# The third value tile, the first queries' load, the bias rows and the order of evictions in the first layer of a two-layer cross-attention kernel

## The chip, the cores and the metric

The kernel runs on one core of a Trainium2 chip. The metric is the device time of one launch in microseconds, lower is better. Five engines work side by side, each with its own queue of instructions in program order: PE (TensorE, matrix products and transposes), ACT (ScalarE), DVE (VectorE), POOL (GpSimd) and SP (SyncE), which here only issues the DMA transfers. They wait for each other on semaphores.

## The reference

Eight batches of 112 query rows and 375 context rows, 512 features each, go through two layers. The change lies wholly in the first, L0:

```
h  = layer_norm(x, ln1_w, ln1_b)
q, k, v = h @ q_w + q_b, ctx @ k_w + k_b, ctx @ v_w + v_b     # 16 heads of 32
o  = softmax(mask(q k^T / sqrt(32))) @ v
x  = x + o @ cproj_w + cproj_b
x  = x + gelu(layer_norm(x, ln2_w, ln2_b) @ fc_w + fc_b) @ proj_w + proj_b
```

The second layer, L1, has 16 heads of 128, two cross-attentions over the same context with one extra key each, and an MLP of its own. All is in f32.

## The kernel before, in words

**Products.** Every product of two f32 matrices is three matmuls (`product`, L1630 to L1632): each operand is kept as a high half (rounded) and a low half (what the rounding left), and high·high, high·low and low·high are summed in PSUM. So each operand that an engine makes is written twice: ACT evicts a PSUM bank with the bias into the `_hi` tile, then DVE computes the `_lo` tile from the same bank and the `_hi` tile. Names: `w_a`, `w_b` weights (slots 0 and 1, loaded into `w_raw_a`, `w_raw_b` in four columns of 128), `cs` the context, `k` a key tile, `v` the values, `act_t` the transposed activations, `x` the rows of the residual (seven tiles of 128).

**Start.** `ln` measures, scales and turns the rows of x. PE meanwhile computes value tiles 0 and 1 of batch 0. Then `query` computes the queries in eight steps i (four columns of the weights, for the first half of the rows and then the second), each evicted by ACT and stored to DRAM by SP (`q_scratch`); from there the queries of each batch are loaded back in another layout. SP, ACT and DVE all have part of that load: SP issues it (L601), ACT makes `q_hi` (L939), DVE makes `q_lo` (L1305). In the `prologue` of the first attention PE computes key tile 0, value tile 2 and key tile 1 of batch 0, the scores of tile 0 and a value tile of batch 1.

**The attention of layer 0** (`attend_first`) runs over eight batches b and four tiles t (four heads each). Everything is software-pipelined by hand. In tile t PE computes the scores of tile t+1 (`score_quad`), and then for each head j = 0 to 3 transposes the probabilities of tile t (`turn`, L1751, into the one bank ps_t) and computes a piece of the keys of tile t+2 or of the values of the next batch (table `FILL`; `FILL_FIRST` in batch 0). At the end comes probabilities times values for the four heads (`weighted`, L1763). ACT evicts each transpose (`turned`, L953), takes the exponential for tile t+1 (`exp`, L957), evicts the key tile (`key_hi`, L947), value tile (`value_out`, L934) and output (`output_hi`, L963). DVE takes scores, mask and maximum (`masked_maximum`, L1336), normalises (`normalized_0`: L1310 and L1313), and makes `k_lo` (`key_lo`, L1319) and the output's low half (L1346). Once a batch, in tile 2, DVE rounds the context of the batch after the next (`context_hi`) and POOL makes its low half in four instructions (`context_lo`, L797).

What each wait is: a `turn` waits until `turned` of the head before it has emptied the bank; `weighted` waits for `turned` of head 3; `score_quad` waits for `key_lo` of its tile and the four maxima of the tile before; key tile 1 waits for `key_lo` of key tile 0, since both use bank ps_k.

The last batch (b = 7) has no next batch to compute keys and values for after tile 1. ACT splits the four columns of the output weights there (`w_b_hi`, POOL makes `w_b_lo`), and PE fills in the first five row tiles of the output projection.

**The tail** (`project` with layer 0) computes row tiles 5 and 6 of the projection, adds to x (`add_y`, L1509), measures, scales (`scale` on DVE, L1199 and L1209), turns (`turn_row`, L1640) and scales the seven rows by the second layer norm (`scaled` on ACT, L878, `halves` on DVE, L1215 and L1217), up to where the MLP starts (`up`). In the last batch the columns of the MLP's first weights (block A_M0) are split as well (`split_hi` on ACT L863, `split_lo` on DVE L1180).

POOL adds the output bias to x (`ln`, L791) as seven instructions in one go after the first layer norm. SP's queue after the last batch: the next block of `w_raw_a`, each column when the same column's `w_lo` is made (`load_block`, L523), then `w_raw_b` for the MLP, the context by key (L714) and the next bias row.

## Time and profile before

| | us |
|---|---|
| median of three runs | 2335.46 (2335.41 to 2336.28) |
| the profiled execution | 2335.53 |
| its span, first to last instruction | 2333.7 |
| PE busy | 2281.2 (98%) |
| DVE busy | 1335.6 (57%) |
| ACT busy | 1123.3 (48%) |
| POOL busy | 366.1 (16%) |

All that the change touches lies in the first 335 us or so of the span. A row of the timeline gives start and duration in us, the engine, the line and operation, output and inputs, and in brackets how long the engine was idle before it and who released it.

### The profile page before, as it was taken

How to read it: one execution, taken by the hardware profiler on the slowest of the kernel's cores; microseconds unless marked ns; L12 is line 12 of the kernel's file. 1: busy time of each engine (PE TensorE's matmuls, PEld its weight loads, DVE VectorE, ACT ScalarE, POOL GpSimd, SP SyncE). 2: the span in 40 equal slices, each digit the busy share in tenths (PEclk: the TensorE clock that was granted, in tenths of full speed). 3: DMA queues.
4: the chain of work that ended last, by engine and by line, in shares of the span. 5: the costliest groups of instructions: out<-in, count | busy, mean ns of one | idle time of the engine just before them, and what ended most of it. 6: DMA issues, size and time to landing. Idle time of an engine off the chain costs nothing.

```text
span 2333.7 us, 37085 instructions
## 1 busy us (share of the span) xinstructions
PE 2281.2 (98%) x13091; PEld 2069.4 (89%) x13091; DVE 1335.6 (57%) x3098; ACT 1123.3 (48%) x2468; POOL 366.1 (16%) x731
## 2 busy tenths in 40 slices
PE   6999899999999999999999999999999999999999
PEld 5777778888999999999998898999999999988887
DVE  6777784443656556655654625665565565554743
ACT  4777762354445445444443434445445444452421
POOL 2111126530000100100101120001001001003421
PEclk9999999999999999999999999999999999999999
DMA  5422126575455645645645474545555555544210
GB/s 180 141 74 71 59 82 229 177 241 144 161 185 196 211 153 197 233 143 193 224 148 164 148 218 153 192 159 193 213 182 182 202 191 190 182 149 139 60 55 32
DMA packets 255224, 376.25 MB, mean 161 GB/s; under 512 B 90302, under 2 KB 210514, under 8 KB 255042
## 3 DMA queue, kind: packets, MB, share of 16 engines
q1 hardware_dynamic: 255042, 373.87, 47.4%
q8 instruction: 108, 1.77, 0.3%
q14 instruction: 74, 0.61, 0.1%
HBM read 315.77 MB, written 58.05 MB: 160 GB/s over the span
## 4 chain that ended last, share of the span: by engine, by line
PE 91%; DVE 3%; ACT 3%; issue 2%; DMA 1%; POOL 0%; SPq 0%; ACTq 0%; DVEq 0%
PE ps_k L1630 10%; PE ps_k L1631 10%; PE ps_k L1632 10%; PE ps_o L1630 8%; PE ps_o L1632 8%; PE ps_o L1631 8%; PE ps_v L1630 6%; PE ps_v L1632 6%; PE ps_v L1631 6%; PE ps_s L1630 4%; PE ps_s L1632 4%; PE ps_s L1631 4%; PE ps_t L1814 3%; PE ps_t L1751 1%; PE ps_o L1763 1%
## 5 line engine op out<-in xcount | busy, mean ns | idle before, releaser
L1630 PE MATMUL ps_k<-cs_hi,w_a_hi 128*128 128x376 f32 x1152 | 390.3, 339 | 3.9 <-DVE k_lo L1405 3.7
L1631 PE MATMUL ps_k<-cs_lo,w_a_hi 128*128 128x376 f32 x1152 | 385.2, 334 | 0.0
L1632 PE MATMUL ps_k<-cs_hi,w_a_lo 128*128 128x376 f32 x1152 | 384.2, 334 | 0.0
L1038 ACT ACTIVATE prob<-ps_s,row_columns 112x376 f32<-112x376 f32 x256 | 147.4, 576 | 304.9 <-DVE row_columns L1411 304.8
L815 POOL CAST k_hi<-xk_hi 128x1 fp32r<-128x1 f32 x256 | 47.4, 185 | 1233.0 <-PE ps_s L1632 1233.0
L1630 PEld LDWEIGHTS ps_k<-cs_hi,w_a_hi 128*128 128x128 f32 x1152 | 216.8, 188 | 7.5 <-issue 6.8
L1631 PEld LDWEIGHTS ps_k<-cs_lo,w_a_hi 128*128 128x128 f32 x1152 | 217.1, 188 | 0.5
L1632 PEld LDWEIGHTS ps_k<-cs_hi,w_a_lo 128*128 128x128 f32 x1152 | 216.9, 188 | 0.0
L1405 DVE SCALAR_TENSOR_TENSOR k_lo<-ps_k,col_b,k_hi 128x375 fp32r<-128x375 f32 x256 | 155.2, 606 | 79.1 <-ACT k_hi L1007 73.5
L1007 ACT ACTIVATE k_hi<-ps_k,col_b 128x375 fp32r<-128x375 f32 x256 | 146.4, 572 | 91.2 <-PE ps_k L1632 90.2
L1310 DVE RECIPROCAL row_columns<-row_columns 112x1 f32<-112x1 f32 x384 | 62.4, 163 | 196.4 <-ACT prob L1038 188.5
L779 POOL TENSOR_TENSOR w_b_lo<-w_raw_b,w_b_hi 128x512 fp32r<-128x512 f32 x84 | 113.1, 1376 | 391.4 <-ACT w_b_hi L863 391.3
L1313 DVE TENSOR_SCALAR prob<-prob,row_columns 112x375 f32<-112x375 f32 x384 | 164.5, 428 | 4.6
L1433 DVE TENSOR_TENSOR sums_lo<-ps_o,sums_hi 128x448 fp32r<-128x448 f32 x128 | 79.9, 625 | 131.0 <-ACT sums_hi L1021 131.0
L1411 DVE TENSOR_REDUCE row_columns<-ps_s 112x1 f32<-112x376 f32 x256 | 138.3, 540 | 8.0 <-PE ps_s L1632 8.0
L1630 PE MATMUL ps_v<-pt_hi,ckd_hi 128*128 128x448 f32 (+1 forms) x384 | 139.9, 364 | 2.2 <-DVE pt_lo L1427 2.2
L1632 PE MATMUL ps_o<-pt_hi,ckd_lo 128*128 128x448 f32 (+1 forms) x384 | 140.6, 366 | 0.0
L1632 PE MATMUL ps_v<-pt_hi,ckd_lo 128*128 128x448 f32 (+1 forms) x384 | 140.6, 366 | 0.0
L1630 PE MATMUL ps_o<-pt_hi,ckd_hi 128*128 128x448 f32 (+1 forms) x384 | 140.3, 365 | 0.0
L1631 PE MATMUL ps_o<-pt_lo,ckd_hi 128*128 128x448 f32 (+1 forms) x384 | 140.0, 365 | 0.0
L1631 PE MATMUL ps_v<-pt_lo,ckd_hi 128*128 128x448 f32 (+1 forms) x384 | 139.9, 364 | 0.0
L1433 DVE TENSOR_TENSOR sums_lo<-ps_v,sums_hi 128x448 fp32r<-128x448 f32 x128 | 80.0, 625 | 101.8 <-ACT sums_hi L1021 101.4
(267 smaller groups left out, 5696.5 us busy)
## 6 DMA issues: line engine op xcount, KB each, us to landing
ckd_hi<-context_by_key_halves SPq DMA_DIRECT2D x64, 768.0 KB, 4.4
ckd_lo<-context_by_key_halves SPq DMA_DIRECT2D x64, 768.0 KB, 6.1
cs_hi<-context_halves SPq DMA_DIRECT2D x64, 752.0 KB, 6.1
cs_lo<-context_halves SPq DMA_DIRECT2D x64, 752.0 KB, 7.8
w_raw_b<-in_blocks_b SPq DMA_DIRECT2D x104, 256.0 KB, 4.5
w_raw_a<-in_blocks_a SPq DMA_DIRECT2D x104, 256.0 KB, 4.8
q<-q_scratch SPq DMA_DIRECT2D x72, 224.0 KB, 6.0
extra<-extra_probability SPq DMA_DIRECT2D x16, 896.0 KB, 4.9
```

The costliest lines, as they stand in the source:

```text
L779: pool.tensor_tensor(w[slot][1][:, :, part], w_raw[slot][:, :, part], w[slot][0][:, :, part], ALU.subtract).then_inc(w_lo[slot], 1)
L1007: act.activation(k[t % 2][0][:, 0:LK], ps_k[:, 0:LK], ACT.Identity, bias=col_b[:, ds(place.column((C_BK0, C_BK1), t), 1)]).then_inc(k_hi, 1)
L1038: act.activation(prob[buf][0:LQ, 0:KW], ps_s[buf][0:LQ, 0:KW], ACT.Exp, bias=max_neg[0:LQ, buf:buf + 1], accum_out=prob_sum[0:LQ, buf:buf ...
L1310: dve.reciprocal(prob_rcp[0:LQ, col:col + 1], prob_sum[0:LQ, col:col + 1]).then_inc(s_rcp, 1)
L1313: dve.tensor_scalar(p[0:LQ, 0:LK], p[0:LQ, 0:LK], prob_rcp[0:LQ, col:col + 1], None, ALU.mult).then_inc(s_norm, 1)
L1405: dve.scalar_tensor_tensor(out=k[t % 2][1][:, 0:LK], in0=ps_k[:, 0:LK], scalar=col_b[:, ds(place.column((C_BK0, C_BK1), t), 1)], in1=k[t % ...
L1411: dve.tensor_reduce(max_neg[0:LQ, t % 2:t % 2 + 1], ps_s[t % 2][0:LQ, 0:KW], AX_X, ALU.max, negate=True).then_inc(s_max, 1)
L1433: dve.tensor_tensor(sums[1][:, d, cols], ps_c[d % 2][:, 0:HALF], sums[0][:, d, cols], ALU.subtract).then_inc(c_lo, 1)
L1630: pe.matmul(out, w_h, m_h, start=first, stop=False)
L1631: pe.matmul(out, w_h, m_l, start=False, stop=False)
L1632: return pe.matmul(out, w_l, m_h, start=False, stop=last)
L1814: last = pe.transpose(ps_t[buf][0:n, i * LQ:(i + 1) * LQ], prob[buf][0:LQ, k0:k0 + n], ident[0:LQ, 0:LQ])
```

## The change

What it does:

- **Value tile.** Value tile 2 of batch 0 is computed and evicted after the transposes of rows 2 and 3 in `ln`, ahead of the queries, and no longer in the prologue between key tiles 0 and 1. Query step 1, which uses the same bank, waits for it (`v_ev` 3).
- **First queries.** SP loads the queries of batch 0 after storing step 4 (before: after step 6). In the prologue ACT and DVE take `split_q` first. DVE makes the low half of the last column of the key weights behind `key_lo` of tile 0, and waits for two of the query stores itself.
- **Bias rows.** POOL adds the output bias to one row tile at the start of each batch 0 to 6, not to seven in one go. In POOL's program the row of batch b+1 stands right behind `context_lo` of batch b, with no wait of its own.
- **Evictions first.** In the tiles of the attention ACT takes `turned` ahead of `key_hi` and of exponentials, in two orders (tile 2, other tiles), and in the last batch as well. DVE takes `key_lo` later by one head.
- **Tail.** The first two standard deviations of the second layer norm move into the last tile. The last column of block A_M0 is split later, behind the measurement of row 6, and DVE scales a row before it adds the next.

The diff, cut to its core:

```
@@ query on SP
-                    if not layer and i == 6:
+                    if not layer and i == 4:
                         for j in range(4):
                             sp.wait_ge(q_out[j], 16)
                         load_q(Place(ATT0, 0, 0, 0, 0))
@@ ln and attend_first on POOL
+                if has_pending(e):
+                    for r in range(RT):
+                        add_bias(r)
+            def add_bias(r):
+                pool.tensor_tensor(x[:, r, :], x[:, r, :], bias_row[:], ALU.add).then_inc(bias_add, 1)
...
+                        if t == 0 and place.b < RT:
+                            add_bias(place.b)
                         if t == 2 and place.after(2):
                             context_lo(place.after(2))
@@ ln and attend_first on ACT
                     scaled(0, 3)
+                    value_out(Place(ATT0, 0, 0, 0, 0), 2)
                     deviation(0, 4)
...
                 def prologue(place):
+                    split_q(place)
                     key_hi(place, 0)
-                    split_q(place)
-                    value_out(place, 2)
                     key_hi(place, 1)
...
+                def tile(place, t):
+                    following = place.key(t + 1)
+                    turned(place, t, 0)
+                    if t == 2:
+                        turned(place, t, 1)
+                        exp(*following, 0)
+                        value_finished(place, t, 0)
+                        turned(place, t, 2)
+                        exp(*following, 1)
+                        turned(place, t, 3)
+                        key_hi(*place.key(t + 2))
+                    else:
+                        exp(*following, 0)
+                        turned(place, t, 1)
+                        exp(*following, 1)
+                        turned(place, t, 2)
+                        key_hi(*place.key(t + 2))
+                        turned(place, t, 3)
+                    exp(*following, 2)
+                    exp(*following, 3)
+                    value_finished(place, t, 3)
+
+                def final_tile(place, t):
+                    following = place.key(t + 1)
+                    for j in range(SUB0):
+                        if not (t == 0 and j == 3):
+                            turned(place, t, j)
+                        if t == 0 and j == 2:
+                            turned(place, t, 3)
+                        if following:
+                            exp(*following, j)
+                        if key_evicted(place, t, j):
+                            key_hi(*key_evicted(place, t, j))
+                        if t == 0:
+                            split_hi(1, place.block_b + 1, (j,), lambda s: (v_mm, 3 * place.batch + 3))
+                        if t == NT - 1 and j == 1:
+                            deviation(1, 0)
+                            deviation(1, 1)
+                    if t == NT - 1:
+                        deviation(1, 2)
@@ attend_first on DVE
                 def prologue(place):
+                    split_q(place)
+                    key_lo(place, 0)
+                    split_lo(0, place.block_a, [NT - 1])
+                    key_lo(place, 1)
                     dve.wait_ge(mask_in_sem, 16)
-                    key_lo(place, 0)
-                    split_q(place)
-                    key_lo(place, 1)
+                    for i in range(2):
+                        dve.wait_ge(q_out[i], 32)
...
                                 masked_maximum(*following, j)
+                                if j == 3 and place.key(t + 2) and (place.final or t == 2):
+                                    key_lo(*place.key(t + 2))
                                 if j:
                                     normalized_0(*following, j - 1)
-                            if key_evicted(place, t, j):
-                                key_lo(*key_evicted(place, t, j))
+                                if j == 2 and not place.final and t != 2:
+                                    key_lo(*place.key(t + 2))
@@ project on ACT
                     scaled(norm, 3)
+                    scaled(norm, 4)
                     deviation(norm, 5)
-                    scaled(norm, 4)
+                    split_hi(0, A_M0, [3], lambda s: (k_mm, NT * NB))
                     deviation(norm, 6)
@@ PE, ln and prologue
                     turn_row(0, 3)
+                    value(first, 2)
...
                     key(place, 0)
-                    value(place, 2)
                     key(place, 1)
```

The order on ACT in tile 3 of a batch (batch 1; `shared` is an evicted transpose, `prob0` to `prob3` the exponentials of the next tile's heads, `k1_hi` the key tile, `v0` the last value tile). Before:

```order
L953 ACTIVATE shared<-ps_t0 128x336
L957 ACTIVATE prob0,row_columns<-prob0,row_columns 112x375
L953 ACTIVATE shared<-ps_t0 128x336
L957 ACTIVATE prob1,row_columns<-prob1,row_columns 112x375
L947 ACTIVATE k1_hi<-ps_k,col_a 128x376
L953 ACTIVATE shared<-ps_t0 128x336
L957 ACTIVATE prob2,row_columns<-prob2,row_columns 112x375
L953 ACTIVATE shared<-ps_t0 128x336
L957 ACTIVATE prob3,row_columns<-prob3,row_columns 112x375
L934 ACTIVATE v0<-ps_v 119x512
```

And now, the same tile:

```order
L960 ACTIVATE shared<-ps_t0 128x336
L964 ACTIVATE prob0,row_columns<-prob0,row_columns 112x375
L960 ACTIVATE shared<-ps_t0 128x336
L964 ACTIVATE prob1,row_columns<-prob1,row_columns 112x375
L960 ACTIVATE shared<-ps_t0 128x336
L954 ACTIVATE k1_hi<-ps_k,col_a 128x376
L960 ACTIVATE shared<-ps_t0 128x336
L964 ACTIVATE prob2,row_columns<-prob2,row_columns 112x375
L964 ACTIVATE prob3,row_columns<-prob3,row_columns 112x375
L941 ACTIVATE v0<-ps_v 119x512
```

The third transpose is evicted ahead of the key tile, and the fourth ahead of the third exponential.

The order on POOL from the second context on. Before:

```order
L797 TENSOR_TENSOR cs_lo<-ctx_raw,cs_hi 128x376 x4
L791 TENSOR_TENSOR x<-x,bias_row 128x512 x7
L797 TENSOR_TENSOR cs_lo<-ctx_raw,cs_hi 128x376 x24
L779 TENSOR_TENSOR w_b_lo<-w_raw_b,w_b_hi 128x4x128 x8
L791 TENSOR_TENSOR x<-x,bias_row 128x512 x7
```

And now:

```order
L801 TENSOR_TENSOR cs_lo<-ctx_raw,cs_hi 128x376 x4
L795 TENSOR_TENSOR x<-x,bias_row 128x512
L801 TENSOR_TENSOR cs_lo<-ctx_raw,cs_hi 128x376 x4
L795 TENSOR_TENSOR x<-x,bias_row 128x512
L801 TENSOR_TENSOR cs_lo<-ctx_raw,cs_hi 128x376 x4
```

Six of the seven bias rows now follow a `context_lo` directly.

On DVE the low half of the last column of A_M0 stood between the last output of the attention and the addition to row 4:

```order
L1346 SCALAR_TENSOR_TENSOR act_t_lo<-ps_o0,col_a,act_t_hi 128x112
L1180 TENSOR_TENSOR w_a_lo<-w_raw_a,w_a_hi 128x4x128
L1509 TENSOR_TENSOR x<-ps_v,x 128x512
L1199 RECIPROCAL row_columns<-row_columns 128x1
L1209 TENSOR_SCALAR shared<-x,mean_var,row_columns 128x512
```

Now it stands behind the addition to row 6 and its measurement, as the 28th instruction behind the last output:

```order
L1558 TENSOR_TENSOR x<-ps_o1,x 128x512
L1227 BN_STATS stats<-x 128x6
L1232 BN_AGGR mean_var<-stats 128x2
L1223 TENSOR_TENSOR w_a_lo<-w_raw_a,w_a_hi 128x4x128
L1242 RECIPROCAL row_columns<-row_columns 128x1
L1252 TENSOR_SCALAR shared<-x,mean_var,row_columns 128x512
```

Whatever SP has queued behind the load of that column now waits for the later place.

## Rows read from the trace of the kernel before

**Rows 1.** The page: busy time, share of the span and instructions of each engine.

```profile
PE 2281.2 (98%) x13091; PEld 2069.4 (89%) x13091; DVE 1335.6 (57%) x3098; ACT 1123.3 (48%) x2468; POOL 366.1 (16%) x731
```

**Rows 2.** Waits of PE, 0 to 500 us: total us, times, longest.

```profile
PE ps_o L1763 <- ACT shared L953: 9.6, 11, 3.2
PE ps_t L1751 <- ACT shared L953: 7.5, 23, 0.4
```

**Rows 3.** Timeline of PE at the start.

```profile
27.17 0.74 PE L1630 MATMUL ps_k<-act_t_hi,w_a_hi 128*128 128x448 f32 x1 [4.56 <-DVE act_t_lo L1217]
...
53.98 0.40 PE L1630 MATMUL ps_v<-w_b_hi,cs_hi 128*119 128x512 f32 x1
...
56.75 0.34 PE L1630 MATMUL ps_k<-cs_hi,w_a_hi 128*128 128x376 f32 x1
```

**Rows 4.** Stretches: length, busy us and instructions by engine, granted clock, DMA.

```profile
27.10:31.80 4.70, 4.63 (x12) 4.03 (x13) 3.69 (x12) 0.54 (x2) 0.00 (x0) 0.50 0.30 88
...
40.85:42.20 1.35, 0.01 (x2) 0.01 (x1) 1.18 (x3) 0.10 (x1) 0.00 (x0) 1.00 0.33 94
...
319.30:322.40 3.10, 3.10 (x9) 2.45 (x8) 2.88 (x8) 1.84 (x6) 0.00 (x0) 0.50 0.91 256
```

**Rows 5.** Timeline of ACT, DVE and POOL around the prologue.

```profile
54.26 0.57 ACT L947 ACTIVATE k_hi<-ps_k,col_a 128x376 fp32r<-128x376 f32 x1 [0.89 <-PE ps_k L1632]
...
53.40 1.84 DVE L1180 TENSOR_TENSOR w_a_lo<-w_raw_a,w_a_hi 128x512 fp32r<-128x512 f32 x1 [1.12 <-ACT w_a_hi L863]
...
55.17 0.60 DVE L1319 SCALAR_TENSOR_TENSOR k_lo<-ps_k,col_a,k_hi 128x376 fp32r<-128x376 f32 x1
...
47.02 11.01 POOL L791 TENSOR_TENSOR x<-x,bias_row 128x512 f32<-128x512 f32 x7
```

**Rows 6.** Timeline of PE, batch 2: end of batch 1, tiles 1, 2, 3.

```profile
123.44 0.79 PE L1763 MATMUL ps_o<-shared,v 128*32 128x112 f32 x24 [0.64 <-ACT shared L953]
...
136.81 0.49 PE L1751 MATMUL ps_t<-ident,prob 112*128 112x112 f32 x3 [0.36 <-ACT shared L953]
...
143.14 0.49 PE L1751 MATMUL ps_t<-ident,prob 112*128 112x112 f32 x3 [0.39 <-ACT shared L953]
...
152.01 0.49 PE L1751 MATMUL ps_t<-ident,prob 112*128 112x112 f32 x3 [0.28 <-ACT shared L953]
...
153.85 0.79 PE L1763 MATMUL ps_o<-shared,v 128*32 128x112 f32 x24 [0.66 <-ACT shared L953]
```

**Rows 7.** Timeline of ACT in tile 3 of batch 2.

```profile
150.97 0.56 ACT L947 ACTIVATE k_hi<-ps_k,col_a 128x376 fp32r<-128x376 f32 x1
151.43 0.44 ACT L953 ACTIVATE shared<-ps_t 128x336 f32<-128x336 f32 x1
```

**Rows 8.** POOL and DVE in tile 2, and the page's group of normalisations (busy us, mean ns).

```profile
142.37 4.10 POOL L797 TENSOR_TENSOR cs_lo<-ctx_raw,cs_hi 128x376 fp32r<-128x376 f32 x4 [26.31 <-DVE cs_hi L1290]
...
144.47 1.14 DVE L1313 TENSOR_SCALAR prob<-prob,row_columns 112x375 f32<-112x375 f32 x1
...
L1313 DVE TENSOR_SCALAR prob<-prob,row_columns 112x375 f32<-112x375 f32 x384 | 164.5, 428 | 4.6
```

**Rows 9.** Timeline of PE in the last batch and the tail.

```profile
283.63 0.79 PE L1763 MATMUL ps_o<-shared,v 128*32 128x112 f32 x24 [3.23 <-ACT shared L953]
...
311.22 1.31 PE L1640 MATMUL ps_t<-ident,prob 128*128 128x128 f32 x8 [0.80 <-DVE prob L1209]
...
318.22 0.66 PE L1640 MATMUL ps_t<-ident,shared 128*128 128x128 f32 x4 [1.96 <-DVE shared L1209]
...
323.57 0.50 PE L1630 MATMUL ps_s<-act_t_hi,w_a_hi 128*128 128x512 f32 x1
```

**Rows 10.** SP's issue and ACT's first use of the MLP's second weights; page: KB, us to landing.

```profile
314.90 2.65 SPq L523 DMA_DIRECT2D w_raw_b<-in_blocks_b  x4
...
333.74 1.14 ACT L863 ACTIVATE w_b_hi<-w_raw_b 128x512 fp32r<-128x512 f32 x2
...
w_raw_b<-in_blocks_b SPq DMA_DIRECT2D x104, 256.0 KB, 4.5
```

More of the change, by code:

```diff
@@ L789, in ln @@
                 pool.wait_ge(bias_in, 16 * e + 16)
-                for r in range(RT):
-                    pool.tensor_tensor(x[:, r, :], x[:, r, :], bias_row[:], ALU.add).then_inc(bias_add, 1)
+                if has_pending(e):
[3 more added lines that the diff above has]
+                pool.tensor_tensor(x[:, r, :], x[:, r, :], bias_row[:], ALU.add).then_inc(bias_add, 1)
             def context_lo(place):
@@ L974, in prologue, with value_finished @@
                             value_out(place.next(), 0)
+                def value_finished(place, t, j):
+                    kind, part = fill(place, t, j)
+                    if kind == VALUE and part[3] == DT:
+                        value_out(*part[0:2])
+                def tile(place, t):
[19 more added lines that the diff above has]
+                    value_finished(place, t, 3)
@@ L976, in one_batch @@
                 def one_batch(place):
                     for t in range(NT):
-                        for j in range(SUB0):
-                            turned(place, t, j)
-                            if place.key(t + 1):
-                                exp(*place.key(t + 1), j)
-                            if key_evicted(place, t, j):
-                                key_hi(*key_evicted(place, t, j))
-                            kind, part = fill(place, t, j)
-                            if kind == VALUE and part[3] == DT:
-                                value_out(*part[0:2])
-                            if place.final and t == 0:
-                                split_hi(1, place.block_b + 1, (j,), lambda s: (v_mm, 3 * place.batch + 3))
@@ L989, in one_batch @@
-                        if place.final and t == NT - 1:
-                            for r in range(3):
-                                deviation(1, r)
+                        if place.final:
+                            final_tile(place, t)
+                        else:
+                            tile(place, t)
                         output_hi(place, t)
-                        if place.split_column(t) is not None:
+                        if place.split_column(t) is not None and not (place.final and t == NT - 1):
@@ L1285, in query @@
                         between(t)
[L1286 removed]
+                    if layer or t < NT - 1:
+                        split_lo(slot, n + 1, [t])
             def context_hi(place):
@@ L1394, in one_batch @@
                         output_lo(place, t)
-                        if place.split_column(t) is not None:
+                        if place.split_column(t) is not None and not (place.final and t == NT - 1):
                             split_lo(0, place.block_a + 1, [place.split_column(t)])
@@ L1534, in scale @@
                         normalized(norm, r)
+                    scale(2)
                     add_y(4, 0, 0)
-                    scale(2)
+                    scale(3)
                     halves(norm, 0)
                     measure(norm, 4)
-                    scale(3)
                     halves(norm, 1)
+                    scale(4)
+                    halves(norm, 2)
+                    halves(norm, 3)
                     add_y(5, 0, 0)
-                    halves(norm, 2)
                     measure(norm, 5)
-                    scale(4)
-                    halves(norm, 3)
+                    halves(norm, 4)
+                    scale(5)
                     add_y(6, 0, 0)
                     measure(norm, 6)
-                    scale(5)
-                    halves(norm, 4)
+                    split_lo(0, A_M0, [3])
                     scale(6)
```

4 lines of the change are left out of this document (1 added, 3 removed).

## The prediction

> **What bounds the kernel now.** I read the page first: PE is busy for 98% of the span [rows 1]. A microsecond counts only where PE waits or runs at half clock. The list of PE's waits says where: in the first 500 us it waits 9.6 us ahead of `weighted` and 7.5 us ahead of `turn`, both for ACT's eviction of a transpose [rows 2]. Then I read PE's timeline at the four places that the change touches. At the start PE idles 4.56 us before the first query [rows 3], and the clock is then 0.50 of full speed for the twelve matmuls of query step 0 [rows 4]. In a batch of the attention it waits four times: 0.36 us in tile 1, 0.39 in tile 2, 0.28 and 0.66 in tile 3; a batch lasts 153.85 - 123.44 = 30.41 us [rows 6]. In the last batch one wait is 3.23 us. In the tail it waits 0.80 and 1.96 us [rows 9], and runs 3.10 us at half clock behind that [rows 4]. These are all that can be won: the rest of the span is matmuls whose number doesn't change.
>
> The profiled execution took 2335.53 us, 1.8 more than its span and within 0.1 of the median 2335.46, so what I take off the span I take off 2335.5.
>
> **Front: value tile 2 into the gap.** The tile takes 56.75 - 53.98 = 2.77 us [rows 3]. The gap runs from 22.61 to 27.17 [rows 3], and what ends it (DVE's low half of row 3) doesn't depend on the tile. PE must first wait some 0.4 us for ACT to empty the bank from value tile 1 (my estimate), so the tile ends near 25.9 and 1.3 us of gap are left. Query 0 starts when it did. At which clock? After 4.56 us of idling it was 0.50: twelve matmuls in 4.65 us [rows 4]. After a gap of 1.35 us, in which PE did nothing, it was still 1.00 [rows 4]. The gap left is like the second, so I take full clock: 4.65 / 2 = 2.3 us earlier. The later steps (transposes of rows 4 to 6, their scaling on ACT, query 4) hang on the end of query 0 and move with it. Ends: 0 if the clock falls anyway, 2.3. I take **2.3**.
>
> **Prologue.** The 2.77 us go, but they were a cover. Key tile 1 may not start before `key_lo` of key tile 0. Key tile 0 ends at 53.98, ACT starts `key_hi` 0.28 later, and it takes 0.57; `key_lo` takes 0.60 [rows 3, 5]. With 0.1 for the semaphores PE now waits 0.28 + 0.57 + 0.60 + 0.1 = 1.55 us bare. Net 2.77 - 1.55 = **1.2**. The queries must be there before that: SP loads them two steps (some 5 us) earlier, so ACT's and DVE's `split_q` fit in while PE computes key tile 0. The split of the last key column behind `key_lo` lies under key tile 1. DVE no longer meets the 11.01 us of bias rows here, under which a column's low half took 1.84 us [rows 5]; if it did, 0.2 less.
>
> **A batch.** A wait in the list counts from the modelled end of the matmul before, but matmuls overlap: the twelve of the value tile started every 0.23 us and last 0.40 each [rows 3]. So each of the four waits is 0.17 longer than listed, and there are two of 0.1 that the list doesn't show: 1.69 + 0.68 = 2.3 us a batch. Now each tile in the new order, with the durations of the rows:
> - Tile 0 has no wait, before and after.
> - Tile 1: the third transpose is evicted ahead of the key tile, so `turn` 3 waits 0.1 where it waited 0.5. Gain 0.4.
> - Tile 2: `turned` 0 and 1 come ahead of the exponential and the value tile; `turn` 2 no longer waits (0.6). But DVE takes `key_lo` behind the fourth maximum, and that behind a normalisation which POOL's `context_lo` holds up (1.14 us where the mean is 0.43 [rows 8]). `key_lo` ends 0.26 us after PE could start the next scores. Net gain 0.3.
> - Tile 3: the eviction at 151.43 stood behind `key_hi` at 150.97 [rows 7] and moves ahead of it: 0.4 us. `weighted`, which waited 0.66 + 0.17, finds the fourth transpose evicted. Gain 1.1, were it not for the bias row.
>
> **The bias row in the attention.** It takes 11.01 / 7 = 1.57 us [rows 5] and now starts when `context_lo` ends, which is when tile 2 ends. `context_lo` is four instructions of 1.03 us from 142.37; their ends are 143.40, 144.42, 145.45, 146.47. The normalisation that started at 144.47 ended at 145.61, 0.16 after one of them [rows 8]: it had waited for POOL's instruction to end, and the column at 53.40 took 1.84 us under a bias row of 1.57 [rows 5]. In the new order the second normalisation ends with the third of these instructions or 0.2 after the fourth has begun, then come the fourth maximum (0.5), `key_lo` (0.6) and a reciprocal, and the third normalisation starts some 0.3 us into the bias row. It would end 0.2 after it: 1.5 us instead of 0.43, so 1.06 late. Behind it on DVE stand the fourth normalisation, the output's low half, the mask and the first maximum of the next batch; ACT's first exponential of tile 3 waits for that maximum, and ACT's second eviction stands behind this exponential, and PE's `turn` 2 waits for the eviction. No slack is on this way, so PE loses **1.0** in tile 3. Ends: 0.3 (the loss that `context_lo` made with a short instruction) and 1.2 (1.84 less what such a column takes alone).
>
> Here the trace and a rule can be weighed. The Trainium skill, SBUF — State Buffer, Who interferes with whom, says that the port pair that DVE and GpSimd share is an exclusive lock, held for a whole instruction by whichever came first. By that rule a normalisation caught at the start of a bias row loses up to 1.57 us, not the 0.7 that it lost under `context_lo`; the sum would be 0.8 us a batch better by the mean of the rows under `context_lo`, and is as I have it by the rule. The end at 145.61 agrees with the rule.
>
> So a batch gains 0.4 + 0.3 + 1.1 - 1.0 = 0.8. Batches 1 to 5 give **4.1**. Batch 6 loads no context and has no bias row: 2.0 of its 2.3. Batch 0: the list has 17.1 us in all; less six batches of 1.69 and the 3.23 that leaves it 3.7 [rows 2, 6, 9]. Tiles 0 and 1 give 1.0 each by the new order, tiles 2 and 3 nothing (collisions as above): **2.0**.
>
> **Last batch.** The fourth transpose is evicted right after the third, so `weighted` at 283.63 comes 1.9 us earlier; but then PE waits for `key_lo`, which stands behind the splits, and in tile 1 for DVE, whose normalisations POOL's `w_b_lo` holds up. **0.8** is left.
>
> **Tail.** The waits of 0.80 and 1.96 [rows 9] go: the first because the square root's table and two deviations move under the last tile, the second because row 3 is scaled ahead of `halves`. Each was 0.17 longer. The half clock behind them (9 matmuls in 3.10 us [rows 4]) goes with the wait in front of it: 1.5. Transposes at the half clock and issue add little. The MLP's first matmul, at 323.57 [rows 9], comes 0.97 + 2.13 + 1.5 = 4.6 us earlier; DVE's `halves` of row 3, which it waits for, allows only 4.1. Then the transposes of rows 5 and 6 wait for DVE, and step 2 waits for ACT, which stands behind the deviation of row 6: 0.8 is given back. **3.3.**
>
> SP's queue: the last column's low half is now made about 11 us later, and SP issues `w_raw_b` of the MLP behind it at 325.6 to 328.2 (in the times of before) where it was 314.90. With 4.5 us to landing it is there at 330 to 332.5; ACT, which took it at 333.74 [rows 10], now wants it near 330.8. I count 0, at worst 2 us of ACT, half of which PE would feel.
>
> **Sum.** 2.3 + 1.2 + 2.0 + 4.1 + 2.0 + 0.8 + 3.3 = 15.7 us, and 2335.5 - 15.7 = **2320**.
>
> **Rivals.**
> 1. *The bias rows cost PE little.* They miss DVE's normalisations, or the ends fall luckily, as happened to some under `context_lo`. Six batches gain up to 0.9 more: 2335.5 - 15.7 - 5.4 = 2314.5. For it: timing of 0.3 us decides it. Against: a row of 1.57 us is hard to miss. 0.20.
> 2. *The clock falls at the start all the same, and the late loads of the MLP hold it.* -2.3 and -3.3 of the sum: 2325.5. For it: the gap of 1.3 us with the value tile before it has no exact like. 0.15.
> 3. *The evictions aren't what the attention waits for.* ACT's exponentials wait for DVE's maxima anyway, so PE waits at the scores instead. Batches gain nothing, and the front clock falls: 2335.5 - 1.2 - 3.3 = 2331, no measurable change (I count within 0.2%, 4.7 us, as none). Against it: the three rows of ACT in a tile show slack. 0.06.
> 4. *Slower: the bias rows stall PE so long that the clock falls.* In the last batch POOL's column splits did this to DVE: PE waited 3.23 us [rows 9]. If a bias row did it in each of six batches, a batch would be 30.41 - 2.3 + 3.23 and, at half clock for as long as in the tail, 1.5 more: 32.8, so 6 x 2.4 = 14.6 lost where I count 6.1 won; the others (9.6) leave 2340. It decides for slower from a stall of 2.9 us, and one bias row makes 1.6 at most. 0.04.
>
> **How the numbers follow.** My forecast has 0.55: 2320, on its own 2317 to 2323. Rival 1 has 0.20, rival 2 0.15, rival 3 0.06, rival 4 0.04. The range 2313 to 2327 takes in the forecast and rivals 1 and 2. Faster by over 0.2%: 0.55 + 0.20 + 0.15 = 0.90; same 0.06; slower 0.04.
>
> **What the profile would show.** Right: query 0 at 27.2 us with clock 1.00 right after; the scores of tile 0 near 55.3 instead of 58.9; no waits for ACT over 0.2 us in tiles 1 to 3, but in tile 3 of batches 1 to 5 one of 0.8 to 1.0 at `turn` 2 and, at the start of tile 3, 0.1 to 0.3 for `k_lo`; a third normalisation of 1.5 us on DVE beside each bias row; the MLP's first matmul near 307 to 309. The prediction is wrong if the clock is 0.50 behind 27.2 us; if the batches last over 30 us or under 29; or if ACT idles for `w_raw_b` or the context by key in the MLP and PE with it.

## The result and the profile after

| | before | after |
|---|---|---|
| median, us | 2335.43 (2334.54 to 2336.28, 6 runs) | 2322.52 (2321.51 to 2324.71, 6 runs) |
| ratio | | 0.9947 (95% interval 0.9934 to 0.9960) |
| the profiled execution, its span | 2335.53, 2333.7 | 2324.71, 2322.9 |

The change is 12.9 us faster by the medians; 15.7 was forecast, and the median lies inside the range, 2.5 us above the forecast. The profiled execution of after is the slowest of its six, so the span alone shows 10.8.

These are PE's waits at the start, in batch 2, in the last batch and in the tail; the rows of before to set beside them are [rows 3, 6, 9]:

```profile
23.04 0.49 PE L1680 MATMUL ps_v<-w_b_hi,cs_hi 128*119 128x512 f32 x1 [0.38 <-ACT v L941]
27.23 0.48 PE L1680 MATMUL ps_k<-act_t_hi,w_a_hi 128*128 128x448 f32 x1 [1.17 <-DVE act_t_lo L1260]
39.68 0.47 PE L1680 MATMUL ps_k<-act_t_hi,w_a_hi 128*128 128x448 f32 x1 [1.04 <-DVE act_t_lo L1260]
53.11 0.41 PE L1680 MATMUL ps_k<-cs_hi,w_a_hi 128*128 128x376 f32 x1 [1.49 <-DVE k_lo L1363]
...
139.75 0.43 PE L1789 MATMUL ps_s<-k_hi,q 32*112 32x376 f32 x2 [0.19 <-DVE k_lo L1363]
144.04 0.49 PE L1802 MATMUL ps_t<-ident,prob 112*128 112x112 f32 x3 [0.67 <-ACT shared L960]
...
268.79 0.79 PE L1814 MATMUL ps_o<-shared,v 128*32 128x112 f32 x24 [1.29 <-ACT shared L960]
270.57 0.43 PE L1789 MATMUL ps_s<-k_hi,q 32*112 32x376 f32 x2 [1.00 <-DVE k_lo L1363]
...
305.95 0.51 PE L1680 MATMUL ps_s<-act_t_hi,w_a_hi 128*128 128x512 f32 x1 [1.20 <-DVE act_t_lo L1260]
309.31 0.66 PE L1690 MATMUL ps_t<-ident,shared 128*128 128x128 f32 x4 [0.32 <-DVE shared L1252]
313.47 0.47 PE L1680 MATMUL ps_s<-act_t_hi,w_a_hi 128*128 128x512 f32 x1 [0.30 <-ACT prob L1186]
324.15 0.42 PE L1680 MATMUL ps_s<-act_t_hi,w_a_hi 128*128 128x384 f32 x1 [2.87 <-ACT prob L1186]
```

The first four rows are the start: value tile 2 stands at 23.04 and the gap ahead of query 0 is 1.17 us instead of 4.56. The next two are the only waits left in batch 2. The last row is new, and it is the one that I had not priced: 2.87 us for ACT in the MLP.

The stretches around the start and the three falls of the clock (length; busy us of PE, weight load, DVE, ACT, POOL; granted clock; DMA share, GB/s):

```profile
27.10:29.40 2.30, 2.17 (x11) 2.03 (x12) 1.92 (x8) 0.54 (x2) 0.00 (x0) 1.00 0.71 210
271.00:274.40 3.40, 3.40 (x22) 2.86 (x17) 3.37 (x6) 1.60 (x4) 1.98 (x2) 0.50 0.01 2
325.50:329.00 3.50, 3.50 (x13) 3.50 (x12) 2.83 (x3) 2.16 (x5) 3.50 (x3) 0.52 0.53 155
1219.80:1223.20 3.40, 3.40 (x10) 3.01 (x11) 0.00 (x0) 0.00 (x0) 0.00 (x0) 0.51 0.85 204
```

Before, the stretch at 27.10 took 4.70 us at 0.50 [rows 4]; now it has the full clock. The fall in the last batch, at 271.00, was in before too (0.53 over 284.90 to 288.50). Instead of the half clock in the tail [rows 4] there is one at 325.5, right behind the new wait, and one at 1219.8 that before does not have. The instructions at 1219.8 are the same in both.

SP's queue and ACT around the new wait (SP: start, length, queue, transfer):

```profile
274.07 37.98 SPq L523 DMA_DIRECT2D w_raw_a<-in_blocks_a  x4
312.09 2.65 SPq L523 DMA_DIRECT2D w_raw_b<-in_blocks_b  x4
314.79 1.09 SPq L714 DMA_DIRECT2D ctx_raw<-in_ctx_by_key  x2
```
```profile
320.91 1.15 ACT L869 ACTIVATE w_b_hi<-w_raw_b 128x512 fp32r<-128x512 f32 x2 [3.13 <-DMA w_raw_b<-in_blocks_b]
322.80 0.63 ACT L1177 ACTIVATE ckd_hi<-ctx_raw 128x512 fp32r<-128x512 f32 x1 [0.75 <-DMA ctx_raw<-in_ctx_by_key]
```

The MLP's second weights are issued from 312.09 to 314.74 and first used at 320.91, 6.2 us behind the end of the last issue. ACT's split waits until all four have landed (`w_in` in `split_hi`); from issue to landing they took 3.6 us at the shortest, 4.1 by the median and 6.8 at the longest. ACT idles 3.13 us for them and 0.75 for the context by key, with a GELU queued behind, and PE waits for that GELU.

### The profile page after: what moved, and what is told of

Read it like the earlier page. It is cut to its first block, busy times and chain, and to the rows that moved or that the text cites. A ratio compares the mean times of both kernels' runs of the same rounds, so it can differ in the third digit from the quotient of the medians.

```text
span 2322.9 us, 37085 instructions
## 1 busy us (share of the span) xinstructions
PE 2278.5 (98%) x13091; PEld 2068.8 (89%) x13091; DVE 1337.1 (58%) x3098; ACT 1123.1 (48%) x2468; POOL 363.4 (16%) x731
## 4 chain that ended last, share of the span: by engine, by line
PE 93%; DVE 3%; ACT 2%; issue 2%; DMA 1%; SPq 0%; DVEq 0%; ACTq 0%
PE ps_k L1680 10%; PE ps_k L1681 10%; PE ps_k L1682 10%; PE ps_o L1680 9%; PE ps_o L1682 9%; PE ps_o L1681 8%; PE ps_v L1680 6%; PE ps_v L1682 6%; PE ps_v L1681 6%; PE ps_s L1680 4%; PE ps_s L1682 4%; PE ps_s L1681 4%; PE ps_t L1864 3%; PE ps_t L1802 2%; PE ps_o L1814 1%
## 5 line engine op out<-in xcount | busy, mean ns | idle before, releaser
L1357 DVE TENSOR_SCALAR prob<-prob,row_columns 112x375 f32<-112x375 f32 x384 | 170.9, 445 | 4.5
```

Of the source, the lines that this page charges most:

```text
L1357: dve.tensor_scalar(p[0:LQ, 0:LK], p[0:LQ, 0:LK], prob_rcp[0:LQ, col:col + 1], None, ALU.mult).then_inc(s_norm, 1)
```

## The experiments

Positions in the traces move as a whole with PE's first instruction, which waits for the first loads: it stands at 9.80 us before, at 9.85 after, and between 9.37 and 10.46 in the experiments. Where I compare positions, I subtract it and say "aligned". The mark that I use most is the start of the MLP's second product, the matmul on `ps_k` at 343.90 before and 332.03 after (aligned: 11.9 us earlier). The executions of one kernel spread over 0.8 to 4 us here, in one case over 6.4, as much as some effects, so each verdict rests on the rows first and on the medians where these can tell.

### The column early again

```
@@ attend_first on ACT and on DVE
-                        if place.split_column(t) is not None and not (place.final and t == NT - 1):
+                        if place.split_column(t) is not None:
@@ project
-                    split_hi(0, A_M0, [3], lambda s: (k_mm, NT * NB))
-                    split_lo(0, A_M0, [3])
```

> The changed kernel with one thing undone: the last column of A_M0 is split where it was before the change (at the end of the last tile, by ACT and DVE); everything else of the tail stays. Theory 'SP queue': the PE wait of 2.87 us at the start of the MLP and the half clock behind it (some 3.4 us of stretch, half of it lost) exist because SP issues the MLP's second weights only behind the late column. Then those weights are issued some 11 us earlier, ACT has no wait for them, the PE wait falls below 0.3 us, the clock stays 1.00 there, and DVE's extra column ahead of row 4 gives back at most 0.5: 4.0 us faster than the changed kernel's 2322.5, so 2318.5 (2317 to 2320.5). Rival 'ACT is behind anyway' (the MLP starts so much earlier that ACT's chain of exponentials of GELU and splits is late without any DMA): the wait stays over 2 us and the time is 2322 to 2323.5.

Measured: 2323.51 us (2320.65 to 2323.95), before on the same chip 2336.16, ratio 0.9943 (0.9929 to 0.9957). The time misses the 2317 to 2320.5 of the theory on SP's queue and is the one that the rival gave (2322 to 2323.5); it is not told from the changed kernel's. The rows say more:

```profile
306.45 0.50 PE L1678 MATMUL ps_s<-act_t_hi,w_a_hi 128*128 128x512 f32 x1 [1.87 <-DVE act_t_lo L1259]
...
307.90 0.63 PE L1680 MATMUL ps_s<-act_t_hi,w_a_lo 128*128 128x512 f32 x1
...
326.72 0.41 PE L1678 MATMUL ps_s<-act_t_hi,w_a_hi 128*128 128x384 f32 x1 [0.28 <-ACT prob L1185]
```

The wait of 2.87 is 0.28, and ACT takes the second weights without idling: about the wait, the theory on SP's queue holds, and the rival, by which it stays over 2 us, is wrong. But DVE's extra column stands ahead of the low half that the MLP's first matmul waits for: 1.87 us instead of 1.20, and behind that the matmuls take 0.63 instead of 0.40 for some 3.5 us. The second product starts 14.9 us earlier than before (aligned), 3.0 better than after, where I expected 4. I priced the column's return at 0.5 and had no fall of the clock in it. The profiled execution, 2320.65, is the fastest of the five; the other four took 2322.42 to 2323.95, and what the 3.0 us were lost to in them is not shown.

### The bias rows in one go

```
                 if has_pending(e):
-                    for r in range(RT):
-                        add_bias(r)
+                for r in range(RT):
+                    add_bias(r)
...
-                        if t == 0 and place.b < RT:
-                            add_bias(place.b)
```

> The changed kernel with GpSimd's seven bias rows in one go behind the first layer norm, as before the change. Theory 'the row holds DVE': the waits of 0.67 to 0.70 us (1.22 in batch 0) ahead of the third transpose in tile 3 are there because DVE's normalisation ends only after the bias row. Then they fall to 0.1 or less in every batch and a batch of 29.33 us lasts 28.6: six batches times 0.75 is 4.5, less 0.2 for rows that meet DVE in the prologue: 2318 (2317 to 2319.5). Rival 'it is the order of the evictions' (ACT's second eviction stands behind the exponential whatever POOL does): the wait stays at 0.5 or more and the time is 2321.5 to 2323.

Measured: 2318.39 us (2316.72 to 2319.68), ratio 0.9921 (0.9909 to 0.9934), 17.8 us below before. The batch length is read on POOL, where `context_lo` starts once a batch:

```profile
105.69 4.12 POOL L800 TENSOR_TENSOR cs_lo<-ctx_raw,cs_hi 128x376 fp32r<-128x376 f32 x4 [24.25 <-DVE cs_hi L1331]
...
219.74 4.12 POOL L800 TENSOR_TENSOR cs_lo<-ctx_raw,cs_hi 128x376 fp32r<-128x376 f32 x4 [24.38 <-DVE cs_hi L1331]
```

(219.74 - 105.69) / 4 = 28.51 us a batch. After has the same marks at 106.11 and 223.43, so 29.33; before at 111.96 and 233.60, so 30.41. In batch 2 PE's wait in tile 3 is gone, and only 0.16 for `k_lo` is left. The theory that the row holds DVE is right, the rival on the order of evictions wrong: a bias row costs 0.82 us a batch and the new orders bring 1.90.

### The front alone, and the evictions alone

The kernel before with the diff's parts on the value tile, the first queries and the prologue:

> The kernel before with the front part of the change alone: value tile 2 ahead of the queries, the first queries' load after step 4, the order of the prologue, the late last column of the key weights. By the terms of the prediction 2.3 (clock) + 1.2 (prologue) = 3.5 faster than 2335.5: 2332.0 (2331 to 2333). The bias rows in one go now run beside the prologue's DVE work, which may cost 0.2. Rival 'the clock gain is given back later' (steps 1 to 7 and the rows' scaling wait for something fixed): 2334 to 2335.5.

Measured: 2333.74 us (2332.73 to 2335.18, 11 runs), ratio 0.9989 (0.9980 to 0.9998): 2.4 us faster, not 3.5, and between the two ranges that were expected. In its profile the last batch's `weighted` starts at 280.14 where before has 283.63 [rows 9], 3.5 earlier. A part is given back right behind it:

```profile
280.10:285.70 5.60, 5.56 (x49) 4.71 (x49) 3.44 (x10) 3.25 (x8) 2.21 (x2) 0.50 0.13 38
```

Before has 0.53 over 3.60 us there (284.90 to 288.50) behind the same wait of 3.23; here it is 0.50 over 5.60. So the steps gained are kept, and 1.0 goes to a longer stretch of half clock at another place. The rival (given back by something fixed in the query steps) is refuted by the 3.5 us at 280.

The kernel before with ACT's `tile` and `final_tile` (without the deviations) and DVE's later `key_lo`, nothing else:

> The kernel before with the orders of evictions in the tiles (ACT) and of the key tile's low half (DVE) alone; front, bias rows and tail are those of before. Theory 'a batch without the bias row gains 1.8': seven batches times 1.8 = 12.6, and 0.8 in the last: 2322 (2320 to 2324), a batch lasts 28.6 us instead of 30.41. Rival 'evictions bring 1.1 a batch, and the bias row costs nothing': a batch lasts 29.3 and the time is 2326 to 2328.

Measured: 2321.78 us (2321.09 to 2321.92), ratio 0.9935 (0.9923 to 0.9948): 14.4 faster. `context_lo` starts at 108.55 and 222.63: 28.52 us a batch. The first theory is right: a batch was put at 28.6 us and the time at 2322. The evictions alone do as much as the whole change.

### SP's order alone

```
                     if place.swap:
-                        load_block(0, place.block_a + 2)
+                        load_block(0, place.block_a + 2, range(3 if place.final else 4))
                         load_block(1, place.block_b + 2)
@@ project on SP, behind the context by key
                     load_by_key_raw(0)
+                    load_block(0, A_M0 + 1, [3])
```

> The changed kernel with SP's queue alone in another order: the load of column 3 of the next block of w_raw_a (the one that waits for the late low half) is issued behind the MLP's second weights and the context by key, not ahead of them; ACT's, DVE's and PE's orders are those of the change. Theory 'SP queue': the second weights go out when the third column's low half is there, near 290, ACT doesn't wait for them, PE's 2.87 us and the half clock behind it (1.6) go, and nothing is given back at the MLP's start, where the late column stays late: 4.4 us faster than the changed kernel, 17 us below the kernel before (ratio 0.9925 to 0.9935). Rival 'the early column gave it all back for another reason than DVE' (as in the run with the column early, whose profile had a fall of the clock at the MLP's start): no more than 1 us better than the changed kernel, ratio 0.9943 or above.

Measured: 2322.03 us (2319.67 to 2323.74), before 2336.27, ratio 0.9937 (0.9925 to 0.9950). That is 14.2 us below before where 17 were expected, and only 0.5 below the changed kernel's 2322.52, which is the rival's "no more than 1 us"; the ratio lies between the two ranges. SP and ACT:

```profile
290.59 2.65 SPq L523 DMA_DIRECT2D w_raw_b<-in_blocks_b  x4
```
```profile
317.48 1.14 ACT L870 ACTIVATE w_b_hi<-w_raw_b 128x512 fp32r<-128x512 f32 x2
```

and PE in the MLP:

```profile
305.78 0.50 PE L1681 MATMUL ps_s<-act_t_hi,w_a_hi 128*128 128x512 f32 x1 [1.19 <-DVE act_t_lo L1261]
309.13 0.66 PE L1691 MATMUL ps_t<-ident,shared 128*128 128x128 f32 x4 [0.31 <-DVE shared L1253]
313.29 0.47 PE L1681 MATMUL ps_s<-act_t_hi,w_a_hi 128*128 128x512 f32 x1 [0.30 <-ACT prob L1187]
326.04 0.42 PE L1681 MATMUL ps_s<-act_t_hi,w_a_hi 128*128 128x384 f32 x1 [0.77 <-ACT prob L1187]
328.20 0.39 PE L1681 MATMUL ps_k<-w_b_hi,cs_hi 128*128 128x512 f32 x1
```

The weights go out 21.5 us earlier, ACT takes them with no idle time, and the MLP's start stays at 1.19. From there to the second product it is 328.20 - 305.78 = 22.42 us, in after 332.03 - 305.95 = 26.08. So the late load costs 3.7 us at this mark in the profile of after: 2.1 of waits (2.87, less the 0.77 that stands ahead of a later step and is there only without the late load) and 1.6 of half clock. In the other profiles with the late load this part of the MLP lasts 25.35 us (after again) and 25.19 (half rows) with the half clock, but 24.08 (bias rows in one go), 24.03 (tail alone) and 23.75 (bias rows in tile 0) without it. The late load thus costs 1.3 to 1.7 us, and 2.8 to 3.7 where the clock falls behind it. The medians show 0.5 us of that here and 2.7 between the two runs with the bias rows in one go (below). Part of the difference is visible: this kernel's profile has the half clock at about 1217 as that of after has it at 1220, and its five executions go from 2319.67, with a mean granted clock of 1.000, to 2323.74, with 0.998.

### The bias rows in tile 0

```
                         if t == 0 and place.b < RT:
+                            pool.wait_ge(t_mm, place.unit + 1)
                             add_bias(place.b)
```

> The changed kernel, but each of GpSimd's bias rows in the batches waits for the first transpose of tile 0, so it runs beside tile 0 and not at the start of tile 3. Number and length of the rows are as in the change. Theory 'only the place of the row costs': the waits of 0.67 to 0.70 us in tile 3 go, tile 0 has no waits to lengthen and hides the held normalisation: 4 to 5 us faster than the changed kernel, like the bias rows in one go (ratio to the kernel before 0.992 to 0.993). Rival 'a row costs PE the same wherever it falls, since DVE has no slack in any tile': no gain, ratio 0.9945 or more, with new waits of 0.5 us in tile 0.

Measured: 2319.36 us (2318.14 to 2321.43), ratio 0.9928 (0.9914 to 0.9941), and 28.52 us a batch (`context_lo` at 106.59 and 220.67). The same rows, as many and as long, cost nothing in tile 0 from batch 1 on; in batch 0 one wait of tile 0 grew from 0.31 to 0.99. By the medians it is 3.2 us below the changed kernel, where 4 to 5 were expected. It is the place that costs, as the first theory had it.

### Both repairs, and the old tail

The bias rows in one go together with SP's order:

> Both repairs: the bias rows in one go behind the first layer norm, and SP's loads of the MLP's second weights ahead of the late column. If the two costs are independent, their gains add up: 17.8 (the bias rows in one go, measured against the kernel before) + 4.4 = 22.2 us below the kernel before, ratio 0.9905 (0.990 to 0.992). If the end of the last batch or the MLP's chain on ACT limits both, it is 0.992 or more.

Measured: 2315.73 us (2315.21 to 2317.69), ratio 0.9911 (0.9898 to 0.9925). This beats both kernels: 20.5 us below before, where 13.8 was measured for the changed kernel in the next group. The 17.8 measured for the bias rows and the 4.4 that were expected (not measured) for SP's order would make 22.2. Against the bias rows in one go alone, SP's order brings 2.7 us by the medians and 1.5 at the mark. The granted clock of 264 to 330 us is 1.00 throughout:

```profile
264.00:330.00 66.00, 60.10 (x403) 49.13 (x404) 56.19 (x116) 43.55 (x104) 19.54 (x14) 1.00 0.24 77
```

The bias rows in one go with the tail of before:

> The changed kernel with the bias rows in one go and the tail of the kernel before (deviations behind the last transposes, column 3 of A_M0 early, DVE adds a row before it scales the one before). It tells what the tail's part is worth. Theory 'the tail's gain and the late loads cancel': PE gets its waits of 0.8 and 2.0 us back (3.3 us slower by the prediction) and loses the wait for the second weights with its half clock (4.4 us faster): within 1.5 us of the run with the bias rows in one go, ratio 0.9915 to 0.993. Rival 'the tail's order brings its 3.3 us net': ratio 0.9935 or more.

Measured: 2318.77 us (2316.84 to 2319.90), ratio 0.9922 (0.9910 to 0.9935), that is 0.4 us from the run with the new tail: gain and late loads cancel. Aligned, the MLP's first matmul stands at 304.66 - 9.37 = 295.3 with the old tail and at 301.56 - 10.21 = 291.4 with the new one and SP's order: 3.9 earlier. At the second product (325.00 and 323.99) only 1.9 of it is left. So even without the late load 2.1 us go back in the MLP; the waits of 0.31, 0.30 and 0.77 above, each some 0.2 longer than listed, make 2.0, and the run with the old tail has none of them. With the bias rows in one go and the new tail the late load itself took 1.7 us, without a fall of the clock, and so the two tails come out within 0.4 us.

### Each bias row as two instructions

```
-                pool.tensor_tensor(x[:, r, :], x[:, r, :], bias_row[:], ALU.add).then_inc(bias_add, 1)
+                pool.tensor_tensor(x[:, r, 0:D // 2], x[:, r, 0:D // 2], bias_row[:, 0:D // 2], ALU.add)
+                pool.tensor_tensor(x[:, r, D // 2:D], x[:, r, D // 2:D], bias_row[:, D // 2:D], ALU.add).then_inc(bias_add, 1)
```

> The changed kernel with each bias row as two instructions of 128x256 instead of one of 128x512; place, order and amount of work are the same. The runs so far show a batch of 29.33 us with the row at the start of tile 3 and 28.51 without it there. Theory 'DVE's normalisation is held until GpSimd's instruction ends': it is now held for a half of 0.65 to 0.8 us only, so the normalisation beside it lasts 0.9 to 1.0 us instead of 1.23, and a batch 28.8 to 29.1; the time is 1.5 to 3 us below the changed kernel's. Rival 'both engines share the memory's bandwidth for as long as GpSimd works': the work is the same, a batch stays at 29.3 and the time is that of the changed kernel within 1 us.

Measured: 2321.62 us (2319.89 to 2321.82), before 2336.37, ratio 0.9934 (0.9921 to 0.9946), and 29.04 us a batch (`context_lo` at 106.31 and 222.49). POOL and then DVE in after, batch 2:

```profile
139.52 1.29 POOL L795 TENSOR_TENSOR x<-x,bias_row 128x512 f32<-128x512 f32 x1
...
139.80 1.22 DVE L1357 TENSOR_SCALAR prob<-prob,row_columns 112x375 f32<-112x375 f32 x1
...
141.13 0.41 DVE L1357 TENSOR_SCALAR prob<-prob,row_columns 112x375 f32<-112x375 f32 x1
```

and with half rows:

```profile
139.46 0.73 POOL L795 TENSOR_TENSOR x<-x,bias_row 128x256 f32<-128x256 f32 x1
140.14 0.84 POOL L796 TENSOR_TENSOR x<-x,bias_row 128x256 f32<-128x256 f32 x1
...
139.73 0.67 DVE L1358 TENSOR_SCALAR prob<-prob,row_columns 112x375 f32<-112x375 f32 x1
...
140.51 0.69 DVE L1358 TENSOR_SCALAR prob<-prob,row_columns 112x375 f32<-112x375 f32 x1
```

In after the normalisation ends at 141.02, 0.21 behind the end of the bias row (140.81). With half rows it ends at 140.40, 0.21 behind the first half (140.19), though POOL works on; the next one, which starts at 140.51 under the second half, ends at 141.20, 0.22 behind that half (140.98). That decides for a hold until GpSimd's instruction ends and against sharing. It is what the Trainium skill says (SBUF — State Buffer, Who interferes with whom: an exclusive lock of the shared port pair), and the trace agrees. The median, 0.9 below the changed kernel's in the same group, is less than the expected 1.5 to 3; the 0.29 us of a batch make 1.7 over six.

### The tail alone, and the changed kernel again

> The kernel before with the tail's part of the change alone (deviations into the last tile, the order of DVE and ACT in the projection, column 3 of A_M0 late). The prediction gave it 3.3 us. Theory 'nothing of it is left': the MLP starts some 4 us earlier, its chain on ACT gives 2.1 back (as between the two runs with the bias rows in one go), and the late loads give 2 to 4 back: between 1 us faster and 2 us slower than the kernel before, ratio 0.9995 to 1.0008. Rival 'the tail alone is worth the predicted 3.3': ratio 0.9986.

Measured: 2336.08 us (2333.99 to 2340.41, 11 runs), ratio 1.0000 (0.9991 to 1.0008). Nothing is left of the tail when it stands alone. The MLP's first matmul comes 3.9 us earlier than in before (aligned), its second product 0.2 us earlier, and no fall of the clock takes part in that: 2.1 us go back as with the bias rows in one go, 1.6 for the late loads. ACT's waits for these are there again:

```profile
333.06 1.15 ACT L863 ACTIVATE w_b_hi<-w_raw_b 128x512 fp32r<-128x512 f32 x2 [1.67 <-DMA w_raw_b<-in_blocks_b]
335.92 0.63 ACT L1137 ACTIVATE ckd_hi<-ctx_raw 128x512 fp32r<-128x512 f32 x1 [1.70 <-DMA ctx_raw<-in_ctx_by_key]
```

> The changed kernel itself once more, beside the others of this group, to tell how much its own time moves between chips and what its profile shows when the waits are the same. Both theories: ratio to the kernel before 0.9940 to 0.9950, a batch of 29.33 us, ACT waits for the MLP's second weights again. If instead the ratio is below 0.993, the differences of 4 us between the other runs and the changed kernel can't be told from its scatter.

Measured: 2322.55 us (2322.16 to 2323.41), ratio 0.9939 (0.9925 to 0.9953), a hair outside the 0.9940 that I had put down, 13.8 us below before. A batch lasts 29.32, ACT waits 2.30 us for the second weights, the half clock behind it is there (323.8 to 327.3), those at 271 and at 1220 aren't. The fall at 271 cost nothing: aligned, the last `weighted` stands at 286.17 with it and at 286.13 here. The runs with the bias rows in one go and in tile 0 lie clearly below this scatter; the ones with the early column, SP's order and half rows do not by their medians alone.

The parts add up. The front alone brings 2.4 us, the evictions alone 14.4, the tail alone 0.3, together 17.1; the changed kernel with the bias rows in one go, which holds all three, has 17.8. The bias rows in the batches take 4.0 of that away and leave the 13.8 of the changed kernel.

## Why the prediction was right, and where it was not

The time lies in the range and the effect is near the sum, 12.9 us for 15.7, but partly by luck: the sum holds two errors that partly cancel. The attention brought more than I took, and the tail, at 3.3 a fifth of the sum, brought nothing (2336.08 against 2336.37 alone). One of my own signs of being wrong came true: ACT idles for `w_raw_b` and the context by key in the MLP, and PE with it. Before's times less after's, at marks:

| part | predicted | measured in the profiles |
|---|---|---|
| front clock | 2.3 | 2.5 (query 4 at 39.68, was 42.20 before) |
| prologue | 1.2 | 1.1 (scores of tile 0 at 55.34, were at 58.91: 3.6 in all) |
| batch 0 | 2.0 | 2.1 (last `weighted` at 87.34, was 93.03) |
| batches 1 to 5 | 4.1 | 5.1 (234.26, was 245.08): 0.8 in batch 1, then 1.08 each (30.41 less 29.33) |
| batch 6 | 2.0 | 2.2 (262.49, was 275.48) |
| last batch | 0.8 | 0.6 |
| to the end of the attention | 12.4 | 13.6 (last `weighted` at 296.02, was 309.63) |
| tail, at the MLP's start | 4.1 | 4.0 (305.95, was 323.57, less 13.6) |
| given back in the MLP | 0.8 | 5.7 (17.6 at its start, 11.9 at the second product) |

**Front clock.** Right: [rows 4] had two gaps, and the gap that is left behaved like the short one, 1.00 in 27.10 to 29.40. Of rival 2 the first half did not happen, its second half (late loads) did, at the predicted size: 3.3 there, 3.7 measured in after and 2.9 in its repeated run.

**Prologue.** Right: the bare wait was given as 1.55 and is 1.49.

**A batch.** The mechanism was right in each tile, the sizes slightly off. Without the bias row the new orders bring 1.90, where 1.8 was predicted (0.4 + 0.3 + 1.1). The row costs 0.82, not 1.0, because it took 1.29 us there where I used 1.57, the mean of seven in a row [rows 5]: the normalisation beside it took 1.22, not 1.5. The waits show where they were forecast, 0.67 (not 0.8 to 1.0) ahead of the third transpose of tile 3 and 0.19 for `k_lo` ahead of it. Five batches: 5.1 instead of 4.1. My list of waits also adds up to less than its parts: 1.69 + 0.68 is 2.4, and 2.6 with the two short ones, not 2.3; the gains by tile don't use it. Rival 4's bound, a stall of 2.9 us, doesn't follow from its terms either: for a loss over 4.7 us they give 3.2. Rival 1 (the rows cost little) was wrong for this place and is true of tile 0.

**Tail.** Its start was right within 0.1. The step that failed is "I count 0, at worst 2 us of ACT, half of which PE would feel". SP's issue time was right: 312.09 and the 13.6 us of the attention make 325.7, where I had 325.6. But I took 4.5 us to landing from the page's median [rows 10], and ACT waits for the slowest of four transfers, the last issued, which took 6.8 here (5.9 in the repeated run, 4.8 in before). ACT idled 3.13 us for the weights and 0.75 for the context by key, nearly twice my worst; PE felt 2.1 us net, about the half that I had said. On top came 1.6 us of half clock, which I had put behind a stall of PE in rival 4 and left out here. Together 3.7 us, and 1.3 to 1.7 where the clock didn't fall. The other 2.1 of the 5.7 are the part that I had at 0.8: an MLP that starts 4 us earlier meets waits for ACT and DVE that the old tail doesn't have. That ACT's deviation, table load and GELU, which did not move, are behind them fits the rows but no run tests it.

**The rest.** From the second product on after should have kept 11.9 and its span shows 10.8. The stretch at 1219.80, nine matmuls at 0.375 instead of some 0.2 us, costs 1.4 and accounts for that. In the repeated run it is absent, and of the 12.7 us that this run has at the second product (aligned) its span keeps 12.6; so it is no effect of the change that I can point to; what makes it appear in some executions stays open.

## What to carry to other kernels

When a step is moved later on an engine, follow the load that waits for it and everything queued behind that load on SP. Here one column's split, moved 11 us later, cost 1.3 to 3.7 us of late loads, and left early it held up the MLP's first matmul by 0.7; an order of SP that issues what is ready first took ACT's wait away at no cost in the rows. A load on which an engine waits as a whole should be priced by its slowest transfer, not by the median of one. A piece of GpSimd work costs by where it stands beside DVE's chain and by how long each instruction is, not by its sum: at the start of tile 3 it cost 0.8 us a batch, cut in two 0.5, in tile 0 or in one go nothing. A wait of PE should be priced with the half clock that can follow it, and an earlier start of a phase with the engine that sets that phase's pace.

## What was unexpected in the hardware

- Where the clock fell did not follow from the listed wait alone. The same two waits of 0.96 and 1.08 us, 1.6 us apart at 1210 to 1232, were followed by some 3.4 us at half clock in five profiles (after, SP's order, evictions alone, the tail alone, and, beginning 0.7 us later, the old tail) and by the full clock in the other eight (before, after again and the bias rows in one go among them).

The first matmul behind the two waits, in the profile of after and in that of the same kernel run again:

```profile
1219.73 0.61 PE L1680 MATMUL ps_v<-pt_hi,ckd_hi 128*128 128x448 f32 x1 [1.08 <-DVE pt_lo L1476]
```
```profile
1219.70 0.47 PE L1680 MATMUL ps_v<-pt_hi,ckd_hi 128*128 128x448 f32 x1 [1.08 <-DVE pt_lo L1476]
```

- The wait for the late load shows the same. Behind 2.87, 2.15 and 1.98 us (after, after again, half rows) the clock fell, behind 2.42, 2.37 and 2.09 (bias rows in one go, the tail alone, bias rows in tile 0) it did not, over the same matmuls. The rows are those of bias rows in one go and of after again:

```profile
319.16 0.41 PE L1677 MATMUL ps_s<-act_t_hi,w_a_hi 128*128 128x384 f32 x1 [2.42 <-ACT prob L1183]
319.20:322.70 3.50, 3.50 (x20) 3.50 (x21) 2.48 (x4) 3.44 (x7) 3.08 (x3) 1.00 0.39 115
```
```profile
323.83 0.66 PE L1680 MATMUL ps_s<-act_t_hi,w_a_hi 128*128 128x384 f32 x1 [2.15 <-ACT prob L1186]
323.80:327.30 3.50, 3.47 (x11) 3.50 (x12) 2.49 (x4) 2.43 (x5) 3.02 (x2) 0.52 0.56 160
```

- How long it stays low differs too: behind the same wait of 3.23 us, 3.60 us in before and 5.60 with the front alone.
- From the last issue to the use of the same four transfers took 6.2 us in after and 4.7 with the bias rows in one go (issued 307.55 to 310.20, used at 314.94), while the page of after gives a median of 4.3 from issue to landing over 104.
- The first loads shift the whole program: PE's first instruction stood between 9.37 and 10.46 us, over a microsecond that no change to the kernel made.
